# Attention on TensorE in phases of three 64-row tiles, with the score-bank fills ahead of the copies

## The chip, the cores and the metric

One core of a Trainium2 chip. The metric is the device time of one execution in microseconds (us), median of the runs. A core has five engines, each with its own in-order list: TensorE (PE in the profile, PEld for its weight loads), VectorE (DVE), ScalarE (ACT), GpSimd (POOL), and SyncE (SP), which starts the DMAs here.

## The reference

Eight sequences of 1024 tokens, 256 wide, go through a mixture of experts, attention, and the mixture of experts again. The change touches attention alone:

```python
q = (c_q @ w_up_q.T).reshape(b, s, H, DH)...      # 16 heads of 64
k, v = ...                                          # from c_kv
q = _apply_rope_subspace(q, DR); k = ...            # rotary, all 64 dimensions
scores = einsum('bhqd,bhkd->bhqk', q, k) * scale
attn = softmax(scores, axis=-1)
out = einsum('bhqk,bhkd->bhqd', attn, v)
out = out.reshape(...) @ w_out.T + residual
```

Everything is fp32. The kernel gets the accuracy of the scores from fp32r products of a high and a low part.

## The kernel before, in words

Attention handles two heads at once (one holds partitions 0 to 63, the other 64 to 127); "head" below means such a pair. There are NN = 64 of them (8 sequences with 8 pairs). Their queries come in two halves t of 512, their keys in 8 blocks j of 128. So a head has 16 tiles (t, j), and a tile has these steps:

- **fill** writes minus the row maxima (SH, brought by a broadcast DMA) into a bank pair PS, so that the scores accumulate on it. ScalarE does it (line 966) for j = 0, 1, 2, 4, 5, 6, VectorE (line 1043) for j = 3 and 7.
- **score** (line 875): three pairs of fp32r matmuls with 64 rows: keys low by queries high, keys high by queries low, high by high. The two matmuls of a pair are the two heads and run side by side on the two halves of TensorE's rows.
- **exp** (line 975, ScalarE; its semaphore is `grown`): PS to PT, one of six buffers.
- **attend** (line 886): PT by V into PO, fp32, 128 rows. After j = 7 ScalarE copies PO to AT (line 982, semaphore `attend_out`), and the next attend with j = 0 waits for that copy.
- **gather** (line 1126, GpSimd): the running sum over keys of PT, in ACC.

A head ahead, **most** (line 854) makes a bank pair of high-by-high scores for head n + 1, and VectorE reduces it to row maxima (line 1037, `most_out`); there are 16 of them in a head too. Scores and mosts share a ring of three PS bank pairs, given out in the order in which TensorE takes them (`ring = Banks(3, ...)`). A most waits for the last reader of its bank, and a score waits for its fill, which waits for that reader.

All other work of TensorE has 128 rows and goes through one bank, OT, one step after the other. A step may start only when the last reader of OT before it is done (`free`, FREED). These steps are **raise** (line 833, queries and keys, four to a head; ScalarE copies OT to R in line 949, then VectorE multiplies OT by the cosines in line 1014), **value** (845, VectorE copies, 1019), **row** (861, ScalarE copies, 960), **sum** (897, ScalarE copies, 987), **outward** (910, VectorE adds, 1066; four of them for two heads, in every second head), and for each eighth head **turn** and **latent** (815, 823). On the way to Q and K stand **sine** (GpSimd, 1105), **rotate** (VectorE, 1027), **high** (ScalarE, 955), **qlow** (VectorE, 1032) and **klow** (GpSimd, 1116).

The list `order` sets the order of everything. All engines walk through it and each does its own part of a step. Before the change it is built in periods of two tiles, eight to a head: two scores, two mosts, steps of the table `early` (the other work), two fills, two attends, gathers, then the tables `late` and `end`.

Of the kernel before, what the change touches and what calls it, by code (L numbers as in the profile page):

```python
# [45 lines left out]
def macaron_kernel(nc, a, out):  # L46
# [4 lines left out]
    T = S // 128  # L51
# [5 lines left out]
    NP = 8  # L57
    GP = 2
    NPT = 6
    NAT = 3  # L60
    NH = 4
    NX = 3
    EPS = 1e-5
# [526 lines left out]
    def attention(src, dst, last_stored):  # L590
        with ExitStack() as local:
            def sb(name, shape, dt):
                return local.enter_context(nc.sbuf_tensor("at" + name, shape, dt))

            def sig(name, by=1):
                return Signal(ctx.enter_context(nc.semaphore("at" + name)), by)
# [21 lines left out]
            RD = [nc.dram_tensor(f"atRD{i}", [2, S], fp32, kind="Internal").ap() for i in range(2)]  # L618
            AT = sb("AT", [128, NAT, S], fp32)
            NM = sb("NM", [128, 2, 2, 4, 2], fp32)  # L620
# [5 lines left out]
            HI = [slice(0, 64), slice(64, 128)]  # L626


            NN = NB * NP
            PER = 8  # L630
            begin, early, late, end = {}, {}, {}, {}

            def at(table, m, period, *steps):

                table.setdefault(PER * (m - 1) + period, []).extend(steps)

            TURNS = [(-21, late), (-20, late), (-17, early), (-17, late), (-9, early), (-9, late), (-8, early), (-8, late)]
            for m in range(NN):
                b, p = divmod(m, NP)
                if p == 0:  # L640
                    names = ("turn", "latent")
                    uses = [(name, b, t, i) for t in range(2) for name in names for i in range(2)]
                    if b == 0:
                        uses = [(name, b, t, i) for name in names for t in range(2) for i in range(2)]
                    for (period, table), use in zip(TURNS, uses):
                        at(table if b else early, m, period if b else -7, use)
                    if b:
                        for i in range(4):
                            at(end, m, -40 + i, ("stats", b, i))
                        for k in range(T):  # L650
                            at(end, m, -33 + k, ("norm", b, k))
                        at(end, m, -36, ("spread", b))
                for k, (i, t) in enumerate(((0, 0), (1, 0), (1, 1), (0, 1))):
                    at(early, m, k - 6, ("raise", m, i, t))
                    at(end, m, k - 5, ("sine", m, i, t))
                    at(late, m, k - 4, ("rotate", m, i, t))
                at(early, m, 0, ("high", m, 1))
                at(end, m, 0, ("high", m, 0), ("klow", m))
                at(early, m, 1, ("value", m, 0))
                at(end, m, 1, ("qlow", m))  # L660
                at(early, m, 6, ("value", m, 1))
                for t in range(2):
                    at(begin, m, 5 + 4 * t, ("minus", m, t))
                    at(late, m, 5 + 4 * t, ("row", m, t))
                    at(end, m, 6 + 4 * t, ("shift", m, t))
                    at(late, m, 14 + 4 * t, ("sum", m, t))
                at(end, m, 19, ("invert", m))
                at(end, m, 20, ("inverse", m))
                at(end, m, 21, ("broadcast", m))
                at(begin, m, 23, ("divide", m, 0), ("divide", m, 1))  # L670
                if p % GP == GP - 1:
                    for u, (period, table) in enumerate([(24, early), (24, late), (27, late), (28, late)]):
                        at(table, m, period, ("outward", m, u))
                if p == NP - 1:
                    for u, period in enumerate((25, 26, 28, 30)):
                        at(end, m, period, ("store", b, u))
                        if b + 2 < NB:
                            at(end, m, period + 3 - u // 2, ("load", b + 2, u))
            at(end, NN - 4, 0, ("next", 0))
            for i in range(4):  # L680
                at(end, NN - 4, 3 + i, ("stats", NB, i))
            for k in range(T):
                at(end, NN - 4, 10 + k, ("norm", NB, k))
            at(end, NN - 4, 7, ("spread", NB))

            order = []
            for g in range(-PER * 2 - 2, PER * NN + 3 * PER):
                n, r = divmod(g, PER)
                t, pair = r // 4, (2 * (r % 4), 2 * (r % 4) + 1)
                scores = [("score", n, t, j) for j in pair] if 0 <= n < NN else []  # L690
                n1, r1 = divmod(g - 1, PER)
                attends = [("attend", n1, r1 // 4, 2 * (r1 % 4) + i) for i in range(2)] if 0 <= n1 < NN else []
                m, q = divmod(g - 1, PER)
                mosts = [("most", m + 1, q, i) for i in range(2)] if 0 <= m + 1 < NN else []
                n2, r2 = divmod(g + 1, PER)
                fills = [("fill", n2, r2 // 4, 2 * (r2 % 4) + i) for i in range(2)] if 0 <= n2 < NN else []
                order += begin.get(g, []) + scores + mosts + early.get(g, []) + fills + attends
                order += [("gather",) + s[1:] for s in attends if s[3] % 4] + late.get(g, []) + end.get(g, [])

            def events(*names):  # L700
                return [step[1:] for step in order if step[0] in names]
# [31 lines left out]
            high = sig("high").expect(events("high"))  # L733
            qlow, klow = (sig(x).expect(events(x)) for x in ("qlow", "klow"))
            valued, value_out = (sig(x).expect(events("value")) for x in ("valued", "valueo"))
            most, most_out = (sig(x).expect(events("most")) for x in ("most", "mosto"))
# [3 lines left out]
            shift = [sig(f"shift{t}", 16).expect(heads) for t in range(2)]  # L740
            filled = [sig(f"filled{i}").expect([s for s in events("fill") if filler(s[2]) == i]) for i in range(3)]
            score, grown = (sig(x).expect(events("score")) for x in ("score", "grown"))
# [8 lines left out]
            def group(n):  # L751

                return n - n % GP + GP - 1
# [34 lines left out]
            def tensor(pe):  # L788
# [16 lines left out]
                for step in order:  # L805
# [94 lines left out]
                    elif name == "outward":  # L900
# [5 lines left out]
                        for i in range(2):  # L906
                            for q in range(GP):
                                for c in range(2):
                                    tok = (2 * u + i) * 128 + 64 * c
                                    ins = pe.eng.matmul(OT[HI[c], i * D:(i + 1) * D], AT[:, (n - GP + 1 + q) % NAT, tok:tok + 64],  # L910
                                                        WO[:, (p - GP + 1 + q) * D:(p - GP + 2 + q) * D],
# [3 lines left out]
            def scalar(act):  # L915
                for step in order:
# [59 lines left out]
                    elif name == "attend":  # L976
                        _, n, t, j = step
                        if j == T - 1:
                            act.wait_ge(*attended(n, t, j))
                            if n >= NAT:  # L980
                                act.wait_ge(*outward(group(n - NAT), 3))
                            act.eng.activation(AT[:, n % NAT, t * 512:(t + 1) * 512], PO[:, :], ACT.Copy).then_inc(attend_out.sem)
                    elif name == "sum":
# [84 lines left out]
            def gpsimd(pool):  # L1068
# [3 lines left out]
                for step in order:  # L1072
# [33 lines left out]
                    elif name == "divide":  # L1106
                        _, n, t = step
                        o = AT[:, n % NAT, t * 512:(t + 1) * 512]
                        pool.wait_ge(*broadcast(n))
# [90 lines left out]

    last_stored = ffn("f1", a["x"], x1, False, True)
    attention(x1, x2, last_stored)
    ffn("f2", x2, out, True, False)

# [61 lines left out]
```

## Time and profile before

| | |
|---|---|
| median of 3 runs | 4242.8 us (4238.97 to 4249.39) |
| the profiled execution | 4230.41 us, its span 4228.6 us |
| TensorE busy | 3947.9 us, 93% of the span |
| GpSimd, VectorE, ScalarE busy | 3032.1, 2965.4, 2772.1 us |
| attention | first qlow at 557.9 us, last one at 3608.3 us |

The first and the last part of the span are the two mixtures of experts, which the change leaves alone. A row of the timeline gives the start, the length, and what ran; "x2" is two instructions together. TensorE's matmuls are pipelined, so the length of a pair (0.40 us) overlaps the next pair, and what a pair costs is the distance between two starts.

### The profile page before, as it was taken

The page shows a single profiled execution, that of the slowest core. Times are in us where ns is not written, and L with a number is a line of the kernel's source. Part 1 is how long each engine was busy: PE and PEld are TensorE (multiplying, and loading weights), DVE is VectorE, ACT ScalarE, POOL GpSimd, SP SyncE. Part 2 cuts the span into 40 slices and gives each one's busy share as a digit, 9 for nine tenths or more (in the row PEclk, how much of TensorE's full clock was granted, in tenths as well). Part 3 has the DMA queues.
Part 4 walks back from the last instruction along what each step waited for, and adds up shares of the span by engine and source line. Part 5 has one row for each costly group of instructions (what it writes and reads, how often), then busy time and mean ns, then how long its engine had stood idle before and what let it go on. Part 6 is the DMA issues. An engine that isn't in the chain of part 4 may idle for free. (4 is left out here: it accounts for less than half of the span.)

```text
span 4228.6 us, 66236 instructions
## 1 busy us (share of the span) xinstructions
PE 3947.9 (93%) x24896; PEld 2236.5 (53%) x24896; DVE 2965.4 (70%) x3707; ACT 2772.1 (66%) x3536; POOL 3032.1 (72%) x1642
## 2 busy tenths in 40 slices
PE   7999979999999999999999999999999999779999
PEld 6888834444444444444444444444444444368888
DVE  5556568777777777777777777777777877455663
ACT  4454457777777776777777777777777777644544
POOL 3444458878888887888888788878887888734444
PEclk9999989999999999999999999999999999989999
DMA  3333221112111211121112112111211122133331
GB/s 107 108 121 111 73 90 61 52 54 82 53 51 59 76 54 57 55 71 52 60 59 68 61 51 72 59 53 56 81 51 51 63 70 62 36 99 116 121 111 61
DMA packets 194224, 301.08 MB, mean 71 GB/s; under 512 B 51470, under 2 KB 102256, under 8 KB 193264
## 3 DMA queue, kind: packets, MB, share of 16 engines
q1 hardware_dynamic: 193904, 296.86, 21.9%
q8 instruction: 196, 3.21, 0.3%
q14 instruction: 124, 1.02, 0.1%
HBM read 201.86 MB, written 26.74 MB: 54 GB/s over the span
## 5 line engine op out<-in xcount | busy, mean ns | idle before, releaser
L1037 DVE TENSOR_REDUCE atNM<-atPS 128x2 f32<-128x1024 f32 x1024 | 1208.0, 1220 | 558.0 <-PE atPS L854 552.7
L1126 POOL TENSOR_TENSOR atACC<-atACC,atPT 128x1024 f32<-128x1024 f32 x512 | 1286.6, 2513 | 69.5 <-ACT atPT L975 15.7
L975 ACT ACTIVATE atPT<-atPS 128x1024 f32<-128x1024 f32 x1024 | 995.8, 1022 | 196.3 <-PE atPS L875 187.8
L886 PE MATMUL atPO<-atPT,atV 128*64 128x512 f32 x4096 | 972.5, 595 | 0.0
L966 ACT ACTIVATE atPS<-atSH 128x1024 f32<-128x1024 f32 x768 | 767.4, 1022 | 37.7 <-DMA atSH<-atMD 22.8
L1126 POOL TENSOR_TENSOR atACC<-atPT 128x1024 f32<-128x1024 f32 x256 | 621.7, 2429 | 107.6 <-PE atOT L897 104.4
L854 PE MATMUL atPS<-atKH,atQH 64*128 64x512 f32 x2048 | 456.5, 448 | 123.8 <-ACT atPT L975 112.2
L1105 POOL TENSOR_TENSOR atVT<-atVT,atSIN 128x512 f32<-128x512 f32 x254 | 332.4, 1309 | 296.6 <-DMA atVT<-atR 296.4
L886 PEld LDWEIGHTS atPO<-atPT,atV 128*64 128x64 f32 x4096 | 282.1, 137 | 474.0 <-issue 467.2
L875 PE MATMUL atPS<-atQH,atKL 64*128 64x512 f32 x2048 | 468.7, 454 | 36.4 <-ACT atPS L966 33.2
L875 PE MATMUL atPS<-atQH,atKH 64*128 64x512 f32 x2048 | 406.3, 392 | 0.0
L875 PE MATMUL atPS<-atQL,atKH 64*128 64x512 f32 x2048 | 405.6, 392 | 0.0
L875 PEld LDWEIGHTS atPS<-atQH,atKL 64*128 64x128 f32 x2048 | 191.8, 184 | 379.9 <-ACT atPS L966 171.1
L854 PEld LDWEIGHTS atPS<-atKH,atQH 64*128 64x128 f32 x2048 | 194.2, 185 | 363.4 <-ACT atPT L975 320.8
L512 POOL TENSOR_TENSOR f2GL<-f2GF,f2GH 128x512 fp32r<-128x512 f32 x144 | 200.9, 1398 | 250.3 <-ACT f2GH L360 245.6
L512 POOL TENSOR_TENSOR f1GL<-f1GF,f1GH 128x512 fp32r<-128x512 f32 x144 | 200.2, 1394 | 250.3 <-ACT f1GH L360 250.3
L1027 DVE TENSOR_TENSOR atU<-atU,atVT 128x512 f32<-128x512 f32 x254 | 360.0, 1417 | 19.8 <-POOL atVT L1105 19.8
L1043 DVE COPY atPS<-atSH 128x1024 f32<-128x1024 f32 x256 | 311.5, 1217 | 11.2 <-ACT atPT L975 11.2
L949 ACT ACTIVATE atR<-atOT 128x512 f32<-128x512 f32 x252 | 150.7, 598 | 182.5 <-PE atOT L833 182.5
L910 PE MATMUL atOT<-atWO,atAT 128*64 128x256 f32 x2048 | 252.5, 390 | 17.1 <-POOL atAT L1111 14.7
L987 ACT ACTIVATE atRSUM<-atOT 128x512 f32<-128x512 f32 x128 | 76.7, 599 | 240.9 <-PE atOT L897 240.9
L468 DVE TENSOR_TENSOR f2GF<-f2HB,f2GB 128x512 f32<-128x512 f32 x128 | 97.1, 758 | 178.9 <-ACT f2HB L354 126.9
(276 smaller groups left out, 6817.3 us busy)
## 6 DMA issues: line engine op xcount, KB each, us to landing
atSH<-atMD SPq DMA_DIRECT2D x128, 512.0 KB, 4.3
atVT<-atR SPq DMA_DIRECT2D x508, 128.0 KB, 2.0
f1GB<-f1GD SPq DMA_DIRECT2D x128, 256.0 KB, 6.8
atRSUM<-atRD SPq DMA_DIRECT2D x128, 256.0 KB, 4.0
f2GB<-f2GD SPq DMA_DIRECT2D x128, 256.0 KB, 6.9
X<-x SPq DMA_DIRECT2D x4, 1024.0 KB, 5.8
XS<-x SPq DMA_DIRECT2D x16, 256.0 KB, 3.9
atRQ<-atRSUM SPq DMA_DIRECT2D x256, 4.0 KB, 1.8
```

The source lines that it names most:

```text
L512: pool.eng.tensor_tensor(GL[n % NH][:, :], GF32[n % NH][:, :], GH[n % NH][:, :], ALU.subtract).then_inc(low_h.sem)
L854: ins = pe.eng.matmul(bank[:, h, :], QH[n % 2][HI[h], q * 128:(q + 1) * 128], KH[n % 2][HI[h], t * 512:(t + 1) * 512], start=True, stop=True)
L875: ins = pe.eng.matmul(bank[:, h, :], kk[HI[h], keys], q[HI[h], sl], start=False, stop=k == 2, skip_group_check=True)
L886: ins = pe.eng.matmul(PO[HI[h], :], V[n % 2][:, j, HI[h]], PT[k % NPT][:, h, :], start=j == 0, stop=j == T - 1)
L910: ins = pe.eng.matmul(OT[HI[c], i * D:(i + 1) * D], AT[:, (n - GP + 1 + q) % NAT, tok:tok + 64], WO[:, (p - GP + 1 + q) * D:(p - GP + 2 + ...
L966: act.eng.activation(PS[ring.of[("score", n, t, j)]][:, :, :], SH[t][:, :, :], ACT.Copy).then_inc(filled[filler(j)].sem)
L975: act.eng.activation(PT[k % NPT][:, :, :], PS[ring.of[step]][:, :, :], ACT.Exp, scale=SCALE).then_inc(grown.sem)
L1027: dve.eng.tensor_tensor(U[:, i, sl], U[:, i, sl], VT[k][:, :], ALU.add).then_inc(rotated.sem)
L1037: dve.eng.tensor_reduce(NM[:, q // 4, :, q % 4, t], PS[ring.of[step]][:, :, :], AX.X, ALU.max, negate=True).then_inc(most_out.sem)
L1043: dve.eng.tensor_copy(PS[ring.of[("score", n, t, j)]][:, :, :], SH[t][:, :, :]).then_inc(filled[2].sem)
L1105: pool.eng.tensor_tensor(VT[k][:, :], VT[k][:, :], SIN[:, t * 512:(t + 1) * 512], ALU.mult).then_inc(sined.sem)
L1126: pool.eng.tensor_tensor(total[:, :, :], begun[:, :, :], PT[k % NPT][:, :, :], ALU.add).then_inc(gathered.sem)
```

## The change

The list is built tile by tile in groups of three: x, x+1 and x+2. Between 128-row work TensorE now has score x, most, score x+1, and further on most, score x+2, most. The attend of tile x-1 stands between these two phases, those of x and x+1 after the second. The steps of the tables keep their places in the head, counted now in ticks of one tile (a period is two ticks; `begin` and `early` belong to the even tick, `late` and `end` to the odd one), and are put in at three places of a group. The fill of a tile stands ahead of the table steps of the tick in every group of steps. `high` of the keys moves one period up, `high` of the queries and `shift` move within theirs, and AT gets a fourth buffer (NAT).

```diff
-    NAT = 3
+    NAT = 4
...
-            begin, early, late, end = {}, {}, {}, {}
+            begin, early, late, end = ((0, 0), {}), ((0, 1), {}), ((1, 0), {}), ((1, 1), {})
...
-                table.setdefault(PER * (m - 1) + period, []).extend(steps)
+                (tick, _), steps_of = table
+                steps_of.setdefault(2 * (PER * (m - 1) + period) + tick, []).extend(steps)
...
-                at(early, m, 0, ("high", m, 1))
-                at(end, m, 0, ("high", m, 0), ("klow", m))
+                at(end, m, -1, ("high", m, 1))
+                at(early, m, 0, ("high", m, 0))
+                at(end, m, 0, ("klow", m))
...
-                    at(end, m, 6 + 4 * t, ("shift", m, t))
+                    at(early, m, 6 + 4 * t, ("shift", m, t))
...
+            def tile(name, x):
+                n, r = divmod(x, 2 * T)
+                return [(name, n, r // T, r % T)] if 0 <= n < NN else []
+            def most_of(x):
+                n, r = divmod(x + 14, 2 * T)
+                return [("most", n, r // 2, r % 2)] if 0 <= n < NN else []
+            def others_of(x):
+                return [step for (tick, _), table in (begin, early, late, end) if tick == x % 2 for step in table.pop(x, [])]
             order = []
-            for g in range(-PER * 2 - 2, PER * NN + 3 * PER):
...
-                order += begin.get(g, []) + scores + mosts + early.get(g, []) + fills + attends
-                order += [("gather",) + s[1:] for s in attends if s[3] % 4] + late.get(g, []) + end.get(g, [])
+            for x in range(-42, 2 * PER * (NN + 4), 3):
+                order += tile("score", x) + most_of(x) + tile("score", x + 1)
+                order += tile("fill", x + 2) + others_of(x) + tile("attend", x - 1)
+                order += [step for step in tile("gather", x - 1) if step[3] % 4]
+                order += most_of(x + 1) + tile("score", x + 2) + most_of(x + 2)
+                if x % T == T - 1:
+                    order += tile("fill", x + 3) + tile("attend", x) + others_of(x + 1) + tile("fill", x + 4) + tile("attend", x + 1)
+                else:
+                    order += tile("fill", x + 3) + others_of(x + 1) + tile("fill", x + 4) + tile("attend", x) + tile("attend", x + 1)
+                order += [step for i in range(2) for step in tile("gather", x + i) if step[3] % 4] + others_of(x + 2)
```

TensorE before, at the end of one head and the start of the next (875 is score, 854 most, 886 attend; the digits behind PS are the bank pair):

```order
L875 MATMUL atPS1<-atQH0,atKL0 128x512 x2
L875 MATMUL atPS1<-atQL0,atKH0 128x512 x2
L875 MATMUL atPS1<-atQH0,atKH0 128x512 x2
L875 MATMUL atPS2<-atQH0,atKL0 128x512 x2
L875 MATMUL atPS2<-atQL0,atKH0 128x512 x2
L875 MATMUL atPS2<-atQH0,atKH0 128x512 x2
L854 MATMUL atPS0<-atKH1,atQH1 128x512 x2
L854 MATMUL atPS1<-atKH1,atQH1 128x512 x2
L886 MATMUL atPO<-atPT2,atV0 64x512 x2
L886 MATMUL atPO<-atPT3,atV0 64x512 x2
```

And TensorE now, near the same place (891 is score, 870 most, 902 attend):

```order
L902 MATMUL atPO<-atPT2,atV0 64x512 x2
L870 MATMUL atPS2<-atKH1,atQH1 128x512 x2
L891 MATMUL atPS0<-atQH0,atKL0 128x512 x2
L891 MATMUL atPS0<-atQL0,atKH0 128x512 x2
L891 MATMUL atPS0<-atQH0,atKH0 128x512 x2
L870 MATMUL atPS1<-atKH1,atQH1 128x512 x2
L902 MATMUL atPO<-atPT3,atV0 64x512 x2
L902 MATMUL atPO<-atPT4,atV0 64x512 x2
L891 MATMUL atPS2<-atQH1,atKL1 128x512 x2
L891 MATMUL atPS2<-atQL1,atKH1 128x512 x2
L891 MATMUL atPS2<-atQH1,atKH1 128x512 x2
L870 MATMUL atPS0<-atKH1,atQH1 128x512 x2
```

Before, the fourth tile of a phase (a most) takes the bank of its first (PS1 twice). Now no bank comes twice in a phase of three, there are more phases, and a phase with one score (the middle one here) has one attend ahead of it.

ScalarE before, around the turn of a query half (975 is exp, 966 fill, 949 the copy to R, 982 the copy of PO, 987 that of the sums):

```order
L975 ACTIVATE atPT4<-atPS1 128x1024
L975 ACTIVATE atPT5<-atPS2 128x1024
L949 ACTIVATE atR1<-atOT 128x512
L966 ACTIVATE atPS2<-atSH1 128x1024
L966 ACTIVATE atPS0<-atSH1 128x1024
L975 ACTIVATE atPT0<-atPS2 128x1024
L975 ACTIVATE atPT1<-atPS0 128x1024
L949 ACTIVATE atR0<-atOT 128x512
L966 ACTIVATE atPS0<-atSH1 128x1024
L982 ACTIVATE atAT<-atPO 128x512
```

And ScalarE now, at the same place (991 is exp, 982 fill, 965 the copy to R, 1003 that of the sums, 998 that of PO):

```order
L991 ACTIVATE atPT3<-atPS2 128x1024
L991 ACTIVATE atPT4<-atPS1 128x1024
L1003 ACTIVATE atRSUM0<-atOT 128x512
L991 ACTIVATE atPT5<-atPS0 128x1024
L982 ACTIVATE atPS2<-atSH1 128x1024
L965 ACTIVATE atR1<-atOT 128x512
L982 ACTIVATE atPS1<-atSH1 128x1024
L991 ACTIVATE atPT0<-atPS2 128x1024
L991 ACTIVATE atPT1<-atPS1 128x1024
L982 ACTIVATE atPS0<-atSH1 128x1024
L965 ACTIVATE atR0<-atOT 128x512
L998 ACTIVATE atAT<-atPO 128x512
```

The copy to R, which stood right behind the exps and ahead of both fills, now stands behind a fill.

## Rows read from the trace of the kernel before

**Rows 1.** Source view of line 1032 (qlow, one to a head), first two rows.

```profile
engine op xcount: duration ns min/median/max, first and last start us, forms
L1032 DVE TENSOR_TENSOR atQL<-atU,atQH x64: 1215/2822/3440, 557.9 to 3608.3; 128x1024 fp32r<-128x1024 f32 x64
```

**Rows 2.** Windows view between these starts: us, then busy us (instructions) by engine, clock.

```profile
557.90:3608.30 3050.40, 2878.42 (x18245) 1333.12 (x18241) 2332.18 (x2447) 2216.80 (x2672) 2508.16 (x1264) 0.99 0.19 60
```

**Rows 3.** TensorE's waits, whole span: us in total, times, longest.

```profile
PE atPS L854 <- ACT atPT L975: 112.2, 433, 0.9
PE atPS L875 <- ACT atPS L966: 33.2, 47, 3.7
...
PE atOT L861 <- DVE atU L1014: 12.3, 18, 2.5
...
PE atOT L897 <- DVE atU L1014: 5.0, 19, 0.4
```

**Rows 4.** Timeline of TensorE, one period: start us, us, engine, line.

```profile
2028.37 0.27 PE L861 MATMUL atOT<-ident,atMC 128*8 128x128 f32 x1
2028.57 0.50 PE L875 MATMUL atPS<-atQH,atKL 64*128 64x512 f32 x2
2028.91 0.39 PE L875 MATMUL atPS<-atQL,atKH 64*128 64x512 f32 x2
...
2030.08 0.40 PE L854 MATMUL atPS<-atKH,atQH 64*128 64x512 f32 x2
2030.65 0.51 PE L854 MATMUL atPS<-atKH,atQH 64*128 64x512 f32 x2 [0.17 <-ACT atPT L975]
2031.09 1.09 PE L845 MATMUL atOT<-atWV,atCKV 128*64 128x128 f32 x16
2032.01 1.89 PE L886 MATMUL atPO<-atPT,atV 128*64 128x512 f32 x8
2033.83 1.07 PE L897 MATMUL atOT<-atACC,atones 128*32 128x512 f32 x8
2034.83 0.50 PE L875 MATMUL atPS<-atQH,atKL 64*128 64x512 f32 x2
```

**Rows 5.** The same in the last head, which has no mosts.

```profile
3655.77 0.39 PE L875 MATMUL atPS<-atQL,atKH 64*128 64x512 f32 x2
3655.99 0.40 PE L875 MATMUL atPS<-atQH,atKH 64*128 64x512 f32 x2
3656.33 1.94 PE L886 MATMUL atPO<-atPT,atV 128*64 128x512 f32 x8
```

**Rows 6.** Timeline of all engines, another period, in part.

```profile
2016.16 0.50 PE L875 MATMUL atPS<-atQH,atKL 64*128 64x512 f32 x2
...
2017.17 1.94 ACT L975 ACTIVATE atPT<-atPS 128x1024 f32<-128x1024 f32 x2 [1.87 <-PE atPS L875]
...
2017.65 0.40 PE L854 MATMUL atPS<-atKH,atQH 64*128 64x512 f32 x2
2018.09 2.36 DVE L1037 TENSOR_REDUCE atNM<-atPS 128x2 f32<-128x1024 f32 x2 [1.13 <-PE atPS L854]
...
2020.29 1.02 ACT L966 ACTIVATE atPS<-atSH 128x1024 f32<-128x1024 f32 x1
2020.43 0.69 DVE L1014 TENSOR_TENSOR atU<-atOT,atCOS 128x512 f32<-128x512 f32 x1
```

**Rows 7.** Groups of the page: line, operation, count | busy us, mean ns | idle before, releaser.

```profile
L1037 DVE TENSOR_REDUCE atNM<-atPS 128x2 f32<-128x1024 f32 x1024 | 1208.0, 1220 | 558.0 <-PE atPS L854 552.7
...
L975 ACT ACTIVATE atPT<-atPS 128x1024 f32<-128x1024 f32 x1024 | 995.8, 1022 | 196.3 <-PE atPS L875 187.8
...
L1027 DVE TENSOR_TENSOR atU<-atU,atVT 128x512 f32<-128x512 f32 x254 | 360.0, 1417 | 19.8 <-POOL atVT L1105 19.8
L1043 DVE COPY atPS<-atSH 128x1024 f32<-128x1024 f32 x256 | 311.5, 1217 | 11.2 <-ACT atPT L975 11.2
L949 ACT ACTIVATE atR<-atOT 128x512 f32<-128x512 f32 x252 | 150.7, 598 | 182.5 <-PE atOT L833 182.5
```

**Rows 8.** ScalarE's waits, whole span: the copy of PO held by outward.

```profile
ACT atAT L982 <- PE atOT L910: 61.4, 31, 2.3
```

More of the change, by code:

```diff
@@ L684, in attention @@
             at(end, NN - 4, 7, ("spread", NB))
-            order = []
-            for g in range(-PER * 2 - 2, PER * NN + 3 * PER):
[L688 to L696, printed above, removed]
-                order += begin.get(g, []) + scores + mosts + early.get(g, []) + fills + attends
-                order += [("gather",) + s[1:] for s in attends if s[3] % 4] + late.get(g, []) + end.get(g, [])
+            def tile(name, x):
+                n, r = divmod(x, 2 * T)
+                return [(name, n, r // T, r % T)] if 0 <= n < NN else []
@@ L700, in events @@
+            assert not any(table for _, table in (begin, early, late, end))
             def events(*names):
```

## Prediction

> **What bounds the kernel now.** I read the busy times by window first. Attention runs in steady state from the first qlow to the last [rows 1]: 3050.4 us for 63 heads, 48.42 us a head. In it TensorE is busy 2878 us, GpSimd 2508, VectorE 2332, ScalarE 2217, at a granted clock of 0.99 [rows 2]. So TensorE sets the pace, with 40, 37 and 35 us a head of work on the others. Then its list of waits: the largest is most for an exp, 112.2 us in 433 waits; the others that matter are score for a ScalarE fill (33.2, 47 times) and two of OT's users for the cosine multiply (12.3 and 5.0) [rows 3]. The timeline of a period gives what a wait really costs, since pairs overlap.
>
> A pair of 64-row matmuls costs 0.23 us. The first of a phase costs 0.34 (2028.57 to 2028.91) [rows 4], and the last, where nothing waits, 0.34 (3655.99 to 3656.33) [rows 5]: 0.11 for each change between 64 and 128 rows, 0.22 a phase. In the period of rows 4 the second most starts 0.57 us behind the first, not 0.23, and the next work 0.44 behind it, not 0.34. That wait is shown as 0.17 of idle time and costs 0.34 + 0.10 = 0.44, so a wait costs its idle time plus about 0.27.
>
> **What the change removes.** The second most of a phase takes the bank whose exp has just begun. With three tiles no bank comes twice in a phase, and an attend (0.91 us, half of 2032.01 to 2033.83 [rows 4]) or more lies between a score and the most that takes its bank. So these 433 waits go: 112.2 + 433 x 0.27 = 229 us. The other 79 of the 512 phases show no such wait (8 have no mosts), though a few lose some tenths; 10 us for them, ends 0 and 20.
>
> The waits for fills and OT (33.2, 12.3 and 5.0 us in 84 waits [rows 3], and about 0.2 for each that overlap hides) come to 67 us. They depend on the order and are counted afresh below, so the 67 us are taken off here. Part of them came from the copy of PO that waited for outward, 61.4 us on ScalarE [rows 8]; the fourth AT buffer ends that, and it is worth nothing else. Taken off in all: 229 + 10 + 67 = 306 us.
>
> **What it adds, first the changes of rows.** 1024 tiles in threes make 341 groups of two phases, 683 phases where there were 512. 171 x 0.22 = 38 us. The Trainium skill has a rule that speaks against the change here: "TensorEngine Tiling (Array Packing)", Key Properties, says that changing the tiling mode drains TensorE. A full drain and refill would be the part of a pair that overlaps its neighbour, 0.40 - 0.23 = 0.17 us each way, and the 171 phases would cost 58 us; the trace has 0.11 each way, and I keep to it.
>
> **Then the fill that is short of time.** In a group the phase with two scores comes first. Call its start 0. The exps begin at 1.01 (2016.16 to 2017.17) and follow each other by 0.92 (two in 1.94, one takes 1.02) [rows 6, 7]. The next fill, for tile x+2, starts behind both at 2.85 and ends at 3.87. With about 0.05 for the semaphore the third score may start at 3.92. (The reduce that it also needs ends at 1.25 + 1.22 = 2.47.) If VectorE fills (one tile in four), it starts behind the reduce at 2.4 and ends at 3.61: 3.66. TensorE gets there after 1.83 (phase: 7 pairs x 0.23 + 0.22), 0.91 (attend) and 0.34 (most) = 3.08, plus the other work that stands between. So it waits 0.84 or 0.58, and a pair behind a wait costs 0.11 more: 0.95 or 0.69.
>
> What stands between is the table step of tick x, and each of the 16 ticks of a head gets into that place once in 16 groups. Raise and value (0.92 each) at six ticks and sum (1.00) at two hide all. Row (0.20) at two leaves 0.75. Outward (1.8) at ticks 0, 1, 7, 9 hides all, in every second head. Ticks 14 and 15 are empty. Head without outward: 4 x 0.95 + 2 x 0.69 + 2 x 0.75 = 6.7 us in 16 groups; with outward 2 x 0.95 + 2 x 0.75 = 3.4. The mean is 0.315 a group, x 341 = 107 us.
>
> **PO's turn.** Once in 24 tiles, 43 times, the attends of j = 7 and of the next j = 0 come in one group with only a table step between. The copy of PO stands behind exp and fill on ScalarE: from the third score's start 1.01 + 0.92 + 0.95 = 2.88, done at 3.48. TensorE wants it at 1.14 + 0.91 = 2.05 plus the step (raise 0.92, outward 1.83, or none): 0.56 in half of the cases, 1.48 or nothing in the others, mean 0.65. 43 x 0.65 = 28 us.
>
> **Copies behind fills.** This has no row of its own. The copy to R takes 0.60 (rows 7) and VectorE's multiply 0.69 (rows 6), and only then is OT free. A raise in the middle place is copied behind a fill, at 2.88 to 3.48, and multiplied until 4.3, while TensorE wants OT at 1.14 + 0.92 + 1.82 = 3.88: 0.4 us, about once a head (four raises, a third of them in that place, most with a step behind). A raise in the first place is copied at 3.8 to 4.4. VectorE's multiply waits for that, and behind it stand two reduces and at times a fill, so that a score gets its bank some 0.5 late. Qlow (median 2.8 us [rows 1]) and the four rotates (1.4 each [rows 7]) push the same reduces back. Following three consecutive heads, one for each position of the groups in a head, I find two to four such waits a head, of 0.3 to 0.6 us. I take 1.4 us a head, 90 us; the ends are 50 (0.8 a head: only the two kinds shown) and 190 (3.0: a wait of 0.55 in each of the 5.3 groups).
>
> **Costed at nothing.** Moving high and shift: high of the keys has half a head more until its first most. The numbers of matmuls and of DMAs stay the same. GpSimd's 40 us a head stay below any head time here. The first and last heads have the same steps and are left at zero, 10 us either way.
>
> **The sum.** -306 + 38 + 107 + 28 + 90 = -43 us, rounded to -41 for the few groups at both ends that are not full. On the profiled execution: 4230.4 - 41 = 4189 us (span and 1.8 us around it). The median of the runs is 12.4 us higher, so 4202 us. Ends of this case: c (the copies) 50 gives 4162; c at 120 gives 4232.
>
> **Rivals.** *The copies cost nothing and fills gain on it.* ScalarE is busy only 35 of 48 us, so a copy could always fit in before the next exp. Then c is 0 and the 79 phases give 20: -141 us, 4102. Against it: VectorE's multiply stands in line behind the copy. Chance 0.18.
>
> *The banks come late in most groups, and the kernel is slower.* Each bank has to pass reduce, fill, score, exp and most in one group of three tiles: 1.22 + 1.02 + 1.0 + 1.02 + 0.5, near 5 us with semaphores, against 8.5 to 9 us for a group. What is left must hold every wait in line on ScalarE and VectorE. If the VectorE multiply that waits for ScalarE's copy (itself behind a fill) delays a reduce and so the next fill by one instruction, 0.95 us, in 60% of the groups, c is 194 us and the time 4306. It decides above c = 131 us, 0.38 a group. For it speak that VectorE has 37 us a head and that half its waits for TensorE vanish; against it that VectorE waits 553 us for mosts in all [rows 7], which is slack. Chance 0.27.
>
> *All of it comes back.* c near 131: 4243, within 0.3%, which is 13 us and about what can be told from no change here. Chance 0.10. *GpSimd paces it:* 2508 of 3050 us busy [rows 2] with the same order of gathers; if its line, not TensorE's, holds the head at 48.4, nothing changes: 4243. Against it: TensorE hardly ever waits for it. Chance 0.06.
>
> **How the numbers follow.** The forecast has 0.39. Faster: 0.38 of it and 0.18 from the first rival, 0.56. Within 0.3%: 0.16. Slower: 0.27 and the forecast's rest, 0.28. The range from 4118 to 4290 takes in most of both rivals; the forecast's own is 4162 to 4232.
>
> **What would show it.** Right: most's wait for exp falls from 433 to a few; score's waits for a ScalarE fill rise from 47 to over 150, at 0.6 to 0.8 of idle time and in the phase with one score; attend waits for the PO copy some 30 to 43 times; the head takes near 47.8 us. Wrong: a head above 48.5 with sum, row or raise waiting for the multiply in hundreds of places, or a head below 46.8 with few waits for fills.

## The result: 1.9% slower, and the profile after

The changed kernel takes 4322.9 us (median of 4 runs, 4317.9 to 4331.3), the kernel before 4240.9 us on the same chip: a ratio of 1.0192 (95% interval 1.0167 to 1.0216), 82 us slower. The forecast was 4202, its range ended at 4290, and slower had been given 0.28. In the profiled executions the spans are 4329.5 and 4228.6 us, 100.9 us apart: 82.8 us of that lie in attention's steady state, 3.4 before its first qlow and 14.7 behind its last. That the 82.8 come so near the 82 of the medians is chance. The source view of qlow, now line 1048, has its first start at 561.3 us and its last at 3694.5:

```profile
L1048 DVE TENSOR_TENSOR atQL<-atU,atQH x64: 1212/2005/3348, 561.3 to 3694.5; 128x1024 fp32r<-128x1024 f32 x64
```

That is 3133.2 us for 63 heads where [rows 1] have 3050.4: 49.73 us a head, 82.8 us more in all. The windows view between these starts:

```profile
561.30:3694.50 3133.20, 2887.22 (x18247) 1312.62 (x18247) 2254.84 (x2447) 2204.06 (x2672) 2513.64 (x1264) 0.98 0.18 59
```

Against [rows 2] TensorE is idle for 246 us, not 172, and busy 9 us longer. VectorE's and ScalarE's busy times fell. TensorE's waits in this stretch (us, times, longest):

```profile
PE atPS L891 <- ACT atPS L982: 136.7, 136, 7.7
PE atPS L891 <- DVE atPS L1059: 21.8, 20, 1.8
PE atPO L902 <- ACT atAT L998: 20.8, 29, 1.3
PE atOT L913 <- DVE atU L1030: 15.6, 22, 1.4
PE atOT L877 <- DVE atU L1030: 13.0, 23, 2.1
...
PE atPS L870 <- ACT atPT L991: 4.5, 10, 0.9
```

Most's wait for an exp, 433 in [rows 3] and 427 between the qlows, is down to 10. In its place score (891) waits for its fill 156 times, 158.5 us, where the kernel before in its own stretch has 33.4 us. What ScalarE's and VectorE's lines waited for, over the whole span:

```profile
DVE atU L1030 <- ACT atR L965: 322.5, 234, 12.7
...
ACT atPS L982 <- DMA atSH<-atMD: 97.7, 49, 8.8
...
ACT atPS L982 <- DVE atNM L1053: 85.8, 127, 3.3
```

The kernel before has 20.6 us, 22.8 us (15 waits) and 7.4 us in these three lines. So fills now wait for two things for which they hardly waited: the row maxima that a DMA brings (SH), all 47 times between 600 and 3650 us those of t = 0, and reduces. And VectorE stands 322 us in front of the cosine multiply, waiting for ScalarE's copy R, which stands behind a fill.

### The profile page after: what moved, and what is told of

Read it like the earlier page. It is cut to its first block and busy times, and to the rows that moved or that the text cites. A ratio compares the mean times of both kernels' runs of the same rounds, so it can differ in the third digit from the quotient of the medians.

```text
span 4329.5 us, 66110 instructions
## 1 busy us (share of the span) xinstructions
PE 3967.7 (92%) x24896; PEld 2221.1 (51%) x24896; DVE 2893.6 (67%) x3707; ACT 2759.4 (64%) x3536; POOL 3033.5 (70%) x1642
## 3 DMA queue, kind: packets, MB, share of 16 engines
q14 instruction: 123, 1.01, 0.1%
## 5 line engine op out<-in xcount | busy, mean ns | idle before, releaser
L1053 DVE TENSOR_REDUCE atNM<-atPS 128x2 f32<-128x1024 f32 x1024 | 1224.7, 1218 | 409.5 <-PE atPS L870 407.6
L991 ACT ACTIVATE atPT<-atPS 128x1024 f32<-128x1024 f32 x1024 | 1015.8, 1023 | 594.1 <-PE atPS L891 583.7
L902 PE MATMUL atPO<-atPT,atV 128*64 128x512 f32 x4096 | 1039.0, 611 | 22.2 <-ACT atAT L998 22.1
L982 ACT ACTIVATE atPS<-atSH 128x1024 f32<-128x1024 f32 x768 | 783.5, 1024 | 186.5 <-DMA atSH<-atMD 97.7
L1142 POOL TENSOR_TENSOR atACC<-atPT 128x1024 f32<-128x1024 f32 x256 | 610.9, 2387 | 205.1 <-PE atOT L913 114.3
L902 PEld LDWEIGHTS atPO<-atPT,atV 128*64 128x64 f32 x4096 | 257.3, 138 | 486.6 <-issue 404.7
L870 PE MATMUL atPS<-atKH,atQH 64*128 64x512 f32 x2048 | 447.3, 433 | 16.3 <-ACT atQH L971 10.3
L1030 DVE TENSOR_TENSOR atU<-atOT,atCOS 128x512 f32<-128x512 f32 x252 | 174.1, 691 | 310.1 <-ACT atR L965 309.7
L1043 DVE TENSOR_TENSOR atU<-atU,atVT 128x512 f32<-128x512 f32 x254 | 292.6, 1152 | 15.1 <-POOL atVT L1121 15.1
L1127 POOL TENSOR_TENSOR atAT<-atAT,atRSUM 128x512 f32<-128x512 f32 x128 | 183.5, 1454 | 67.1 <-DMA atRSUM<-atRD 66.9
```

The source lines that it names most:

```text
L870: ins = pe.eng.matmul(bank[:, h, :], QH[n % 2][HI[h], q * 128:(q + 1) * 128], KH[n % 2][HI[h], t * 512:(t + 1) * 512], start=True, stop=True)
L902: ins = pe.eng.matmul(PO[HI[h], :], V[n % 2][:, j, HI[h]], PT[k % NPT][:, h, :], start=j == 0, stop=j == T - 1)
L982: act.eng.activation(PS[ring.of[("score", n, t, j)]][:, :, :], SH[t][:, :, :], ACT.Copy).then_inc(filled[filler(j)].sem)
L991: act.eng.activation(PT[k % NPT][:, :, :], PS[ring.of[step]][:, :, :], ACT.Exp, scale=SCALE).then_inc(grown.sem)
L1043: dve.eng.tensor_tensor(U[:, i, sl], U[:, i, sl], VT[k][:, :], ALU.add).then_inc(rotated.sem)
L1053: dve.eng.tensor_reduce(NM[:, q // 4, :, q % 4, t], PS[ring.of[step]][:, :, :], AX.X, ALU.max, negate=True).then_inc(most_out.sem)
```

## The experiments

Ratios are to the kernel before on the same chip, with 95% intervals. "After" is the changed kernel, 1.0192.

**Row first.** After, with the maxima of t = 0 ahead in SyncE's list:

```diff
+ for m in range(NN):
+     row_, raise_, shift_ = ("row", m, 0), ("raise", m + 1, 0, 1), ("shift", m, 0)
+     # SyncE only: row_ goes ahead of raise_
+     # and ("broadcast", m - 2) behind shift_
```

> The changed kernel with one difference, in SyncE's list alone: the DMA of the row maxima of t = 0 stands ahead of the swap of the last raise (it stood behind it and so behind the rotate that the swap waits for), and the broadcast of the sums behind that of the maxima. The first theory is that the maxima arrive late: in the changed kernel's trace ScalarE's fills wait 97.7 us for them in 49 waits, nearly all for t = 0, where the kernel before has 22.8 us in 15. If it holds, those waits fall to about 10 us in under 15 waits, TensorE's idle time for ScalarE fills falls from 142 to about 70 us, and the time from 4323 to about 4245. If instead the chain exp, exp, fill on ScalarE is what is short (second theory), TensorE waits at the same places anyway and the time falls by at most 15 us, to 4308.

1.0112 (1.0093 to 1.0132): 34 us of the 82. From 600 to 3650 us, ScalarE's waits for maxima fell from 88.1 us in 47 to 15.5 us in 16, TensorE's for ScalarE fills from 125.3 us in 131 to 95.9 us in 128. Less than the 78 us expected: some of the fills that no longer wait for maxima now wait for a reduce, a line that rose from 83.7 us to 106.0. Late maxima are a cause, and not the only one. What the wait looks like is in the timeline of after:

```profile
2216.40 0.27 PE L877 MATMUL atOT<-ident,atMC 128*8 128x128 f32 x1
...
2218.48 0.25 ACT L976 ACTIVATE atML<-atOT 8x128 f32<-8x128 f32 x1
...
2219.56 1.13 SPq L1166 DMA_DIRECT2D atVT<-atR  x2
...
2220.79 0.43 SPq L1171 DMA_DIRECT2D atMD<-atML  x1
2221.26 1.13 SPq L1199 DMA_DIRECT2D atRSUM<-atRD  x2
2222.55 0.47 SPq L1177 DMA_DIRECT2D atSH<-atMD  x1
...
2228.13 1.97 ACT L982 ACTIVATE atPS<-atSH 128x1024 f32<-128x1024 f32 x2 [2.24 <-DMA atSH<-atMD]
2229.21 0.50 PE L891 MATMUL atPS<-atQH,atKL 64*128 64x512 f32 x2 [2.29 <-ACT atPS L982]
```

Row runs on TensorE at 2216.40; ScalarE copies it at 2218.48, behind a fill; SyncE sends it at 2220.79, because the swap of the last raise (line 1166) stands ahead and waits for a rotate; the maxima land 5.6 us after the last issue, and fill and score wait 2.3 us. From row to the moment at which ScalarE is ready for that fill were 9.5 us. The same head of the kernel before (row at 2171.24) has 9.5 us too, but its DMA goes out 4.3 us after the row, not 6.2, and nothing waits. All heads show both sides of it: in the kernel before the room is 9.4 us or more in all 62 and the DMA goes out 4.4 us after the row on average; in the changed kernel the room is 7.0 to 7.3 us in 17 heads of 61, and the DMA goes out after 5.3 us.

**No wait for maxima.** After, with all fills reading a constant (left out: the subtraction of the maxima; the exponent is scaled down by 1000):

```diff
- act.wait_ge(*shift[t](n)) ... SH[t][:, :, :]
+ act.wait_ge(*made(1))     ... SC_[:, :, :]     # zeros
```

> The changed kernel in which the fills read a constant buffer of zeros that is ready from the start, and the exponent is scaled down by 1000 so that it stays finite; the maxima are still reduced and broadcast, but no fill waits for them (left out: the subtraction of the maxima). It bounds what late maxima cost. First theory: 4323 - 80 = 4243 us, and equal to the run with the row ahead within 10 us. Second theory (the ScalarE chain is short of time by itself): no less than 4305. Whatever remains over the 4241 of the kernel before comes from fills that are short of time, PO's turn, and OT.

1.0061 (1.0045 to 1.0077). Late maxima cost 55 us in all, two thirds of the loss. The rest, 26 us over the kernel before, is there with every maximum on time: score still waits 103.5 us for fills in 134 waits (600 to 3650 us; after has 147.1 in 151). Both theories were partly right. The 55 us hold some 16 us of clock, which came back with the waits (see "The clock").

**Copies first.** After, with each tick's fills behind its table steps:

```diff
-  order += tile("fill", x + 2) + others_of(x) + tile("attend", x - 1)
+  order += others_of(x) + tile("fill", x + 2) + tile("attend", x - 1)
   # and both fills of the second place behind others_of(x + 1)
```

> The changed kernel with the fills behind the table steps of their tick in each of the three places, so that ScalarE's copies stand ahead of the fills again (one half of the change undone). If copies behind fills are what costs (the fall-back theory of the prediction: OT waits), the waits of sum, row, value and outward for OT, 52 us of idle time, shrink to 20 and the time falls by 30 to 50 us to about 4280. If the fills are what is short, each copy of 0.6 us now delays a third-score fill, and the time rises by 20 to 60 us to about 4365.

1.0532 (1.0514 to 1.0549), 144 us slower than after. Waits for OT nearly went (9.6 us from 600 to 3650), waits for fills rose to 280 us. In groups of three the fills are what is short, more than I had expected; the copies are the cheaper ones to delay.

**The split.** The kernel before, with the second most behind the first attend:

```diff
-  scores + mosts + early.get(g, []) + fills + attends
+  scores + mosts[:1] + early.get(g, []) + fills + attends[:1] + mosts[1:] + attends[1:]
```

> The kernel before with one difference: the second most of each period stands behind the first attend. No bank comes twice in a phase, periods stay two tiles long, and fills keep their place. It tests the two terms that the prediction took as sure: the 433 waits for exp go (-229 us) and 512 phases more are paid (+113 us). If both are right and no new wait comes up: 4241 - 116 = 4125 us. If a wait for exp is only exchanged for one for fills, since the period's length is set by the chain on ScalarE and VectorE, it is 4241 or more.

0.9932 (0.9915 to 0.9948): faster, the waits for exp all gone, but 29 us and not 116. The timeline gives the main reason, the price of a phase:

```profile
2007.58 1.03 PE L886 MATMUL atPO<-atPT,atV 128*64 128x512 f32 x4
2008.54 0.50 PE L854 MATMUL atPS<-atKH,atQH 64*128 64x512 f32 x2
2008.97 1.08 PE L886 MATMUL atPO<-atPT,atV 128*64 128x512 f32 x4
2009.88 1.90 PE L910 MATMUL atOT<-atWO,atAT 128*64 128x256 f32 x16
...
2015.39 0.50 PE L854 MATMUL atPS<-atKH,atQH 64*128 64x512 f32 x2
2015.82 1.08 PE L886 MATMUL atPO<-atPT,atV 128*64 128x512 f32 x4
2016.83 0.27 PE L861 MATMUL atOT<-ident,atMC 128*8 128x128 f32 x1
```

The most takes 0.43 for 0.23 of work (0.20 for the two changes). The attends beside it cost more as well. The one ahead of it takes 0.96, the one behind it 0.91 ahead of outward and 1.01 ahead of row (2015.82 to 2016.83), sum or score. In the kernel before a pair of attends takes 1.71 to 1.72 ahead of outward and 1.82 ahead of row or sum:

```profile
3172.02 1.89 PE L886 MATMUL atPO<-atPT,atV 128*64 128x512 f32 x8
3173.73 1.90 PE L910 MATMUL atOT<-atWO,atAT 128*64 128x256 f32 x16
```

So two attends cost 0.15 more with a most between them, in both cases. A phase costs 0.35, not the 0.22 of the prediction, and 512 more cost about 180 us. Against the 219 us that the waits for exp were worth (below) that leaves some 40. Waits for ScalarE fills rose too, from 32.6 us in 45 to 63.2 in 61 between the qlows. That would leave under 10 us where the stretch became 34 us shorter, so these prices hold to some 30 us and no better.

**Multiply later.** Row first, with VectorE's multiply on R and behind the next reduce:

```diff
-  dve...tensor_tensor(U[:, i, sl], place(step), COS[:, sl], ALU.mult)
+  dve...tensor_tensor(U[:, i, sl], R[swap_of(n, i, t)[0]][:, :], COS[:, sl], ALU.mult)
-  FREED = {... "raise": cosine,
+  FREED = {... "raise": raw,
+  act.wait_ge(*cosine(*before))     # ScalarE, ahead of the next copy into the same R
```

> The changed kernel with the row's DMA ahead (as in the run before), and with VectorE's cosine multiply reading R, ScalarE's copy, in place of OT, and standing behind the next reduce. So OT is free after ScalarE's copy, and no reduce waits behind a multiply that waits for that copy. The theory for what is left over the kernel before (ratio 1.011): VectorE idles 302 us behind the multiply's wait, reduces come late, and ScalarE's fills wait 106 us for them. If so, fills waiting for reduces fall from 106 to under 50 us, TensorE's idle time for fills from 118 to under 85 us and for OT from 32 to under 10, and the ratio to the kernel before is 0.995 to 1.000. The rival, that the fills are short because ScalarE runs exp, exp, fill one after the other: fills wait on TensorE as before and the ratio stays at 1.006 to 1.011. The multiply may also get slower by reading two operands of SBUF beside GpSimd (0.69 to 1.4 us, as the rotate), which would hide a part.

1.0272 (1.0252 to 1.0291), slower than row first by 68 us. The caveat decided: the multiply takes 1447 ns on average where it took 691.

```profile
L1041 DVE TENSOR_TENSOR atU<-atR,atCOS 128x512 f32<-128x512 f32 x240 | 347.2, 1447 | 2.9 <-ACT atR L966 2.9
```

Its waits for R vanished, but VectorE's busy share rose from 74% to 79%, and ScalarE fills waited 187.9 us for reduces. As a test of who stands behind whom it is inconclusive. It suggests that VectorE's line is close to the pace: four multiplies a head, each 0.76 us longer, went with 1.1 us more a head. But the run also moved the multiply and made ScalarE's copy wait for it, so the 1.1 us are not shown to be VectorE's time alone.

**Fills first in the kernel before.** The second half of the change alone:

```diff
-  scores + mosts + early.get(g, []) + fills + attends
+  scores + mosts + fills + early.get(g, []) + attends
```

> The kernel before with its fills ahead of the other steps of the period, and nothing else: the second half of the change alone. In periods of two tiles a phase comes 4.3 us or more after the last and the fills have some slack, so little moves: the 47 waits for ScalarE fills (33 us) fall to half and OT waits rise. Theory that fills first is good in itself: ratio 0.995. Theory that it only mends what three-tile groups need: 0.999 to 1.003. That putting copies first cost 144 us in groups of three says only that fills are critical there.

1.0572 (1.055 to 1.0594): far outside both expectations. In periods of two tiles both fills stand together, so a copy waits for two, VectorE's multiply for the copy, and row, sum and outward for OT, in every period that has a raise. The waits for exp stay (600 to 3600 us):

```profile
PE atPS L854 <- ACT atPT L975: 112.5, 447, 0.8
PE atOT L861 <- DVE atU L1014: 55.2, 57, 1.4
PE atOT L897 <- DVE atU L1014: 51.1, 56, 1.4
PE atOT L910 <- DVE atU L1014: 49.2, 54, 1.5
PE atOT L897 <- DVE atV L1019: 40.9, 57, 1.2
```

Where fills have slack, a fill ahead of a copy costs 5.7%; where they have none, a copy ahead of a fill costs 3.3%.

**Split, with four AT and the row first.** The split plus `NAT = 4` and SyncE's list of the first experiment:

> The kernel before with the second most behind the first attend (ratio 0.993 by itself), four AT buffers, and the row's DMA ahead on SyncE. In the run with the split alone ScalarE waited 46 us for maxima and 79 us for the outward that holds AT, and TensorE 57 us for fills. If those waits are the cause of TensorE's, they fall by 30 to 40 us and the ratio is 0.984; if TensorE's fills wait for exps and reduces, 0.992.

0.9855 (0.9837 to 0.9874), 4176.3 us, the fastest of all: 3.3% under the changed kernel. TensorE waits 36.5 us for ScalarE fills in 44 waits (600 to 3600 us), where the split alone has 56.8 in 59. The same with the fills first as well:

> As the run before it, with the fills also ahead of the other steps of the period. If fills are short of time in the split order too, 0.980; if VectorE's multiply then waits behind ScalarE's fills and holds back the reduces, as in groups of three, 0.990 or more.

1.0369 (1.035 to 1.0389): in the range of the second theory, but mainly for the reason of the fills-first run. OT waits for the multiply and V's copy are 152 us; the reduces held back, of which that theory speaks, show as 20.7 us of most's waits (600 to 3600 us).

**Most next.** The kernel before, with the second most opening the next phase:

```diff
-  order += begin.get(g, []) + scores + mosts + early.get(g, []) + fills + attends
+  order += held + begin.get(g, []) + scores + mosts[:1] + early.get(g, []) + fills + attends
+  held = mosts[1:]
```

> The kernel before with the second most of a period moved to the head of the next phase: most, score, score, most. One phase a period as before, and the most no longer follows 0.6 us behind the score whose exp holds its bank. Against the split order (ratio 0.993) it saves 512 phases, which the traces price at 0.22 (row changes) to 0.30 us (with the attend beside the change): 113 to 154 us. But the closing most takes the bank of the opening one, whose reduce (1.22 us, begun 0.5 us after the opening) ends just when the bank is asked for, at 1.8: a wait of 0.1 to 0.3 us. If the phases are what the split order paid with: 4236 - 229 + 50 to 100 = about 4080, ratio 0.955 to 0.975. If the wait for exp only turns into one for the reduce because VectorE is late (0.5 us and more, in 450 waits), 0.995 or more.

1.0161 (1.0144 to 1.0178). The wait for exp turned into one for the reduce, as the rival said, and the ratio lies in its range (0.995 or more). From 600 to 3600 us:

```profile
PE atPS L855 <- DVE atNM L1038: 200.3, 156, 2.8
PE atPS L876 <- ACT atPS L967: 19.4, 27, 1.9
```

VectorE comes to that reduce late, from a rotate or fill before it. The waits are 156 and not the rival's 450, but long; over all phases with 128-row work behind them, the closing most starts 0.48 us (median) behind the last score pair, where pairs follow each other in 0.23. With four AT and the row first:

> As the run above, with four AT buffers and the row's DMA ahead on SyncE, which together were worth 0.008 in the split order (0.993 to 0.9855). The faster the periods, the later the maxima and AT: 0.008 to 0.015 below the run above.

1.0185 (1.0168 to 1.0202), no gain at all. The wait for the reduce stayed (212.5 us in 157 waits), and an earlier DMA does not touch it.

**Four AT alone.**

> The kernel before with four AT buffers alone, a part of the change. The prediction held it worth nothing by itself. ScalarE's 61 us of waits for outward go. If TensorE's waits for ScalarE fills (33 us, and 0.27 more for each of 47) came in part from them: ratio 0.994 to 0.997; if not, 0.999 to 1.001.

0.9977 (0.9966 to 0.9988), a gain of 10 us, between the two answers. The expectation misquotes the prediction, which held the fourth buffer to end the waits for outward and to be worth nothing beyond that, with those waits among the 67 us that it took off. A gain of 10 us agrees with it.

**Third fill on VectorE.** Row first, with `filler(n, t, j)` returning VectorE for the third tile of each group and ScalarE for the two others, j = 3 and 7 among them:

> The changed kernel with the row's DMA ahead (ratio 1.011), in which VectorE makes the fill of each group's third score, and ScalarE the two others: 341 fills on VectorE where there were 256. It tells apart two theories for the fills that are still short. First: ScalarE runs exp, exp, fill, and the third score is asked for before that is over (3.08 us against 3.92). A fill on VectorE, behind one reduce, ends at 3.66, beside the exps, and the wait shrinks by 0.26 us in the 256 groups where it was ScalarE's, some 30 to 60 us: ratio 0.997 to 1.004. Second: VectorE is late with what stands in its line (multiplies that wait for ScalarE's copy, rotates, qlow), and 85 fills more there (1.2 us each, 100 us of work) make it later: TensorE's waits for VectorE fills rise from 22 to over 100 us and the ratio to 1.02 or more.

1.0093 (1.0076 to 1.0109), near the 1.0112 of row first. Waits moved and did not go: ScalarE fills 95.9 to 23.0 us, VectorE fills 21.8 to 72.4 us, sum's for OT 20.9 to 47.8 (600 to 3650 us). Neither theory alone: work taken off ScalarE's line and put on VectorE's shortened waits in the one and lengthened them in the other.

## Why the prediction was wrong

**Right.** The removed wait and its size: 433 waits to 10, idle 111.1 to 4.5 us between the qlows, with 0.27 hidden in each -219 us (forecast -229). The 0.27, read from one period, holds: over 426 of these waits in the kernel before the distances between starts give 0.26 each. PO's turn: 29 waits, 20.8 us and 0.27 each, 29 us (forecast 28). The signs it named for being right were there, except the head time. The one for being wrong was there in that time alone (49.7 us, over 48.5): sum, row or raise waited for the multiply in 47 places, not hundreds. Waits for OT, the term held most uncertain, came out below the forecast: 53.6 us of idle time after, 22.1 before, +32 us, where 66 were expected (90 less the 24 of OT in what was taken off). It came out lower because much of what copies behind fills cost showed as fill waits, not because the term was well sized.

**The step that failed: "Costed at nothing".** It gave the move of shift no price since the transfers stay the same in number. The time at which each transfer is asked for did not stay the same. I had read how often fills waited for the maxima, not how much room they had. The no-maxima run puts late maxima at 55 us, of which the row's DMA of t = 0 ahead gives back 34. A group of three brings a fill up to two ticks nearer to the row before it, the copy of the row stands behind a fill, and its DMA behind a swap that waits for a rotate.

**The fill term was too small without that.** It counted the chain exp, exp, fill: 107 us in 128 waits (6 groups of 16). The no-maxima run has 134 waits and 103.5 us of idle time, 140 us with the hidden 0.27. The chain did not count that the reduce is late too, by the multiply that waits for R: 301 us of VectorE's time in that run as well. That this wait is what makes the reduces late is argued from the order of the lists; the run that was to test it, multiply later, did not. The term for copies had an entry for it, 0.5 us a time, as an OT wait; it comes out as fill waits, longer.

**Phases cost more.** From after's timeline, an attend between two phases:

```profile
2203.76 0.39 PE L891 MATMUL atPS<-atQH,atKH 64*128 64x512 f32 x2
...
2204.08 1.08 PE L902 MATMUL atPO<-atPT,atV 128*64 128x512 f32 x4
2205.09 0.49 PE L870 MATMUL atPS<-atKH,atQH 64*128 64x512 f32 x2
...
2222.62 1.08 PE L902 MATMUL atPO<-atPT,atV 128*64 128x512 f32 x4
2223.63 0.50 PE L870 MATMUL atPS<-atKH,atQH 64*128 64x512 f32 x2
```

1.01 us, not the 0.91 of half a pair [rows 4]; behind a raise it is 0.96. 341 such attends at 0.05 to 0.10 are about 25 us, an estimate, beside the 38 forecast: some 63 for 171 phases more, 0.37 each, where the split gives 0.35. The change of rows is paid in part in the matmul that stands beside it, which the prediction had not read. The Trainium skill ("TensorEngine Tiling (Array Packing)", Key Properties) says that a change of the tiling mode drains TensorE, without a price. The prediction's estimate of such a drain by the overlap, 0.17 us each way and 58 us in all, was nearer than the 38 to which I kept.

**The clock.** Left out altogether. Its mean over the span fell from 0.984 to

```profile
core 0: 4329.5 us, clock 0.975
```

In windows of 10 us between 590 and 3690 us, 21 of 310 lie below 0.9 (before: 6 of 301), and what is missing to full clock sums to 43 us against 10. It goes with the waits for fills: 31 us in row first, 26 in no maxima, 84 in copies first. One of the windows, after a long wait:

```profile
1119.49 0.50 PE L870 MATMUL atPS<-atKH,atQH 64*128 64x512 f32 x2
1124.05 0.79 PE L891 MATMUL atPS<-atQH,atKL 64*128 64x512 f32 x2 [4.06 <-ACT atPS L982]
1124.64 0.63 PE L891 MATMUL atPS<-atQL,atKH 64*128 64x512 f32 x2
1125.07 0.63 PE L891 MATMUL atPS<-atQH,atKH 64*128 64x512 f32 x2
```

The granted clock from 1124 to 1129 us is 0.50, the lower level of 1.2 GHz, and pairs take 0.43 us instead of 0.23. In the kernel before the 433 waits were short (0.9 us at most); now there are fewer and longer ones. About 30 us. This is read from the traces; no run held the clock apart.

**The sum again**, before to after, in us between the qlows: exp waits -219; fills +154 (idle +125, hidden +29); PO +29; OT +32; phases +38; lone attends +25; clock about +30. Together +89, measured +82.8. The nearness says less than it seems: 0.27 hidden in each of 56 more OT waits would be another 15 us, and the phases are not measured by themselves in this kernel. Forecast were -239, +64, +28, +66, +38, 0 and 0. So the miss comes from fills above all (90 us, about half of it late maxima), then from the clock (30), the attends (25) and the wait removed (20), less 34 for OT.

**The rival.** The slower rival had the mechanism (banks late in line, a fill a whole instruction late in many groups) and 4306 us; it lacked the maxima and the clock, and there were 156 late fills in 341 groups, not one in 60% of them. That its time came so near is in part luck. It had been given 0.27, against the forecast's 0.39, although both sides of the sum were near 300 us and one side had been read while the other was estimated.

**Open.** How the last 26 us (no-maxima against before) divide between ScalarE's chain and late reduces: multiply later was spoilt by the slower multiply, third fill on VectorE moved the waits. That maxima first would help the kernel before by itself was not run.

## What to carry to other kernels

A wait in an in-order list that is short and regular can be the cheap one. Before it is taken out, measure the slack of every other chain that the new order shortens, the DMA chains too: from the step that starts them to the one that wants them. Then change the smallest thing (here one most, one place later, with one DMA moved and a fourth AT buffer: 1.5% faster), and treat "fills before copies" as a property of one schedule: the same edit was worth 3.3% in one order and cost 5.7% in the other.

## What the hardware showed that was not expected

- The cosine multiply on 128x512 fp32 took 0.69 us with one operand in PSUM and 1.45 us on average with both in SBUF (0.67 to 2.88), beside a GpSimd that is busy 82% of the time.
- Two 128-row attends took 0.15 us more with a 64-row phase between them (1.87 for 1.72 us ahead of outward, 1.97 for 1.82 ahead of row or sum), on top of 0.20 us in the phase itself.
- After a 4 us wait of TensorE its granted clock was 0.50 for 5 us, and pairs cost 0.43 us where they cost 0.23.
